# Two normalisation stages of a two-layer network, their orders of work written anew

## The reference, cut to what matters

```python
m = jnp.mean(x, axis=channels); v = jnp.var(x, axis=channels)
xn = (x - m) / jnp.sqrt(v + eps)                          # normalise, eps 1e-6
x_proj = jnp.einsum('bchw,mc->bmhw', xn, w_in)            # 128 -> 16 channels
s = x + xn
...                                                       # FFT, gain, inverse FFT of x_proj: x_enh (16 channels)
x1 = s + jnp.einsum('bmhw,cm->bchw', x_enh, w_out)        # 16 -> 128 channels
tn = (x1 - mean(x1)) / jnp.sqrt(var(x1) + eps)            # eps 1e-5
total[c, b] = sum over the points of tn                   # for the router of the experts
```

## Time and profile before

| | |
|---|---|
| median of three runs | 3659.25 us (3657.81 to 3667.75) |
| the profiled execution's own time | 3660.29 us |
| its span, first to last instruction | 3658.5 us |
| TensorE busy, share of the span | 87% |
| VectorE, ScalarE, GpSimd | 46%, 42%, 22% |
| mean granted TensorE clock | 0.903 of full |

### The profile page before, as it was taken

The page is one execution under the profiler, slowest core; times in us unless marked ns, Lnnn a source line. Parts: engine busy times, 40 slices in busy tenths (PEclk is TensorE's granted clock), DMA queues, the critical chain, the costliest instruction groups (busy, mean ns, idle before and its releaser), DMA issues. The chain is left out here.

```text
span 3658.5 us, 67013 instructions
## 1 busy us (share of the span) xinstructions
PE 3166.6 (87%) x27077; PEld 1711.9 (47%) x27136; DVE 1684.6 (46%) x2348; ACT 1527.2 (42%) x2263; POOL 810.3 (22%) x694
## 2 busy tenths in 40 slices
PE   5655676399999985999997879999999999999999
PEld 1155422255555542566665434546463545545444
DVE  5724256567677541111112254545454645545453
ACT  3411244167776661111223334545453444445433
POOL 2410232134444421111110112121212111121221
PEclk7767666699999985999998889999999999999999
DMA  5421364313334323777777311313132231313000
GB/s 187 154 75 23 121 257 196 157 46 138 147 147 164 153 115 123 187 212 214 214 207 236 123 56 52 127 46 128 51 104 81 76 109 41 110 43 125 12 12 23
DMA packets 192538, 438.59 MB, mean 120 GB/s; under 512 B 33341, under 2 KB 100157, under 8 KB 183741
## 3 DMA queue, kind: packets, MB, share of 16 engines
q1 hardware_dynamic: 192356, 436.20, 35.9%
HBM read 247.40 MB, written 188.75 MB: 119 GB/s over the span
## 5 line engine op out<-in xcount | busy, mean ns | idle before, releaser
L2113 DVE TENSOR_TENSOR d_hid_scaled<-d_hid_scaled,d_ps 128x512 f32<-128x512 f32 x512 | 331.3, 684 | 605.7 <-PE d_ps L1800 553.6
L1789 PE MATMUL d_ps<-d_hid_scaled,d_w 128*128 128x512 f32 x1024 | 526.4, 596 | 8.0 <-DVE d_X L2119 3.8
L1974 ACT ACTIVATE d_hid_scaled<-d_ps,d_b 128x512 f32<-128x512 f32 x512 | 349.9, 686 | 382.0 <-PE d_ps L1778 375.6
L1517 PE MATMUL c_ps<-c_pad,c_weight 32*32 32x512 f32 x13824 | 475.2, 601 | 26.2 <-ACT c_pad L1469 18.9
L1517 PEld LDWEIGHTS c_ps<-c_pad,c_weight 32*32 32x32 f32 x13824 | 287.1, 103 | 214.1 <-issue 129.7
L1776 PE MATMUL d_ps<-d_tnh,d_w1h 128*128 128x512 f32 x512 | 296.5, 579 | 9.2 <-ACT d_hid_scaled L1974 9.2
L1148 PE MATMUL b_ps<-b_hid,b_w2s 128*128 128x512 f32 x512 | 261.6, 595 | 0.0
L2061 POOL CAST d_tnh<-d_TN 128x512 fp32r<-128x512 f32 x64 | 39.9, 623 | 972.7 <-PE d_ps L1778 935.4
L1578 DVE COPY c_pad<-c_P 128x1024 f32<-128x1024 f32 x48 | 33.4, 696 | 414.9 <-PE c_ps L1517 379.2
L1789 PEld LDWEIGHTS d_ps<-d_hid_scaled,d_w 128*128 128x128 f32 x1024 | 195.5, 191 | 44.5 <-DVE d_hid_scaled L2113 2.3
L1469 ACT ACTIVATE c_pad<-c_P 128x1024 f32<-128x1024 f32 x48 | 51.8, 1080 | 392.7 <-PE c_ps L1517 372.0
(11 more groups left out here) (270 smaller groups left out, 5858.7 us busy)
## 6 DMA issues: line engine op xcount, KB each, us to landing
scratch_qkv<-b_qkv SPq DMA_DIRECT2D x64, 768.0 KB, 3.5
c_P<-scratch_qkv SPq DMA_DIRECT2D x192, 256.0 KB, 4.7
scratch_agg<-c_out SPq DMA_DIRECT2D x192, 256.0 KB, 5.0
d_buf<-scratch_qkv SPq DMA_DIRECT2D x96, 512.0 KB, 4.4
d_buf<-scratch_agg SPq DMA_DIRECT2D x96, 512.0 KB, 3.8
p_X<-in_x SPq DMA_DIRECT2D x8, 2048.0 KB, 7.5
scratch_s<-p_X SPq DMA_DIRECT2D x8, 2048.0 KB, 6.3
m_X<-scratch_s SPq DMA_DIRECT2D x8, 2048.0 KB, 7.7
```

Source lines behind the costliest of these rows:

```text
L1517: end = nc.tensor.matmul(ps[on(i), k * QUADS + h, :].rearrange("p (b r w) -> p b r w", b=2, w=HB), weight[k][on(q), 2 * r + x, on(h)], pad ...
L1789: nc.tensor.matmul(moe_bank, w2[:, e, :], scaled[n % 3][:, :], start=False, stop=(e == E - 1)).then_inc(moe_pe, 1)
L1974: nc.scalar.activation(hid[n % 3][:, :], hid_bank(n), ACT.Gelu, bias=b1[:, n % E:n % E + 1]).then_inc(hid_done, 1)
L2113: nc.vector.tensor_tensor(scaled[n % 3][:, :], hid[n % 3][:, :], spread_bank(n), ALU.mult).then_inc(scaled_done, 1)
```

## The change

Both stages get new orders; the arithmetic is the same. In the projection stage the squares have eight buffers; `variances` is cut in two halves that stand behind `cast_inverse` 0 to 3 and 4 to 7, `means(b+1)` stands behind both, and `project` and `read` work on image b-2 and stand last; ScalarE does `deviations` before `split(b+1,0)`; VectorE does all eight `scale` before `invert`. In the mix stage `X` and `XE` hold four images; `mix` runs two images ahead and in pairs between the groups of casts and sums; `means(b+1)` stands behind the first four `cast_mean(b)`; `split(b-1,1)` and `join(b-1,1)` move to the next turn, the join behind `centre(b)`; `join(b+1,0)` stands before `invert(b)`. SyncE loads four images ahead, and stores `x1` of b+2 in turn b.

```diff
 # projection stage
-        norm = TileNorm(nc, ctx, "p_norm", ..., [t[:, :] for t in banks[2:6]])
+        norm = TileNorm(nc, ctx, "p_norm", ..., [t[:, :] for t in banks[2:6]], NCH)
...
                     for c in range(NCH):
                         norm.cast_mean(pe, b, c, mean_free(b))
+                    for c in range(4):
+                        norm.cast_inverse(pe, b - 1, c, inverse_free(b - 1))
+                    norm.variances(pe, b, range(4))
+                    for c in range(4, NCH):
+                        norm.cast_inverse(pe, b - 1, c, inverse_free(b - 1))
+                    norm.variances(pe, b, range(4, NCH))
                     if more:
                         means(b + 1)
-                    for c in range(4):
-                        norm.cast_inverse(pe, b - 1, c, inverse_free(b - 1))
-                    norm.variances(pe, b)
-                    for c in range(4, NCH):
-                        norm.cast_inverse(pe, b - 1, c, inverse_free(b - 1))
-                    project(b - 1)
+                    if b >= 2:
+                        project(b - 2)
...
                 body(B - 1, False)
                 for c in range(NCH):
                     norm.cast_inverse(pe, B - 1, c, inverse_free(B - 1))
+                project(B - 2)
                 project(B - 1)
...
                     for c in range(NCH):
                         norm.squares(act, b, c, xn_part(b), lambda c: norm.wait_centred(act, b, c))
+                    norm.deviations(act, b, eps)
                     if more:
                         norm.split(act, b + 1, 0)
-                    norm.deviations(act, b, eps)
                     norm.split(act, b, 1)
+                    if b >= 2:
+                        read(b - 2)
...
                 for b in range(1, B - 1):
                     body(b, True)
-                    read(b - 1)
...
                     centre(b)
-                    scale(b - 1, range(6))
+                    scale(b - 1, range(NCH))
                     norm.invert(dve, b)
-                    scale(b - 1, range(6, NCH))
 # mix stage
-        X, TN, XE = sb("X", [128, 3 * HW]), sb("TN", [128, 3 * HW]), sb("XE", [128, 3 * ROWS])
+        X, TN, XE = sb("X", [128, 4 * HW]), sb("TN", [128, 3 * HW]), sb("XE", [128, 4 * ROWS])
...
                 load(0)
-                for b in (1, 2):
+                for b in range(1, 4):
                     sp.wait_ge(loaded, b * 80)
                     load(b)
                 store_x1(0)
...
+                sp.wait_ge(x1_stored, 16)
+                store_x1(1)
+                for b in range(B):
+                    if b + 4 < B:
+                        next_load(b)
+                    if b + 2 < B:
+                        sp.wait_ge(x1_stored, b * 16 + 32)
+                        store_x1(b + 2)
+                    if b:
+                        store_tn(b - 1)
...
+                for b in range(2):
+                    for i in range(NCH):
+                        mix(b, i)
+                    if b == 0:
+                        means(0)
+                def mixes(b, some):
+                    for i in some:
+                        if b < B:
+                            mix(b, i)
+
+                for b in range(B):
+                    for c in range(4):
                         norm.cast_mean(pe, b, c, mean_free(b))
-                        if more:
-                            mix(b + 1, c)
...
+                    if b + 1 < B:
+                        means(b + 1)
+                    mixes(b + 2, (0, 1))
+                    for c in range(4, NCH):
+                        norm.cast_mean(pe, b, c, mean_free(b))
+                    mixes(b + 2, (2, 3))
+                    if b:
+                        for c in range(4):
+                            norm.cast_inverse(pe, b - 1, c, inverse_free(b - 1))
+                    mixes(b + 2, (4, 5))
+                    norm.variances(pe, b)
+                    mixes(b + 2, (6, 7))
+                    if b:
+                        for c in range(4, NCH):
+                            norm.cast_inverse(pe, b - 1, c, inverse_free(b - 1))
                 for c in range(NCH):
                     norm.cast_inverse(pe, B - 1, c, inverse_free(B - 1))
...
+                for b in range(B):
+                    if b:
+                        norm.split(act, b - 1, 1)
+                    squares(b, (0, 1))
+                    if b + 1 < B:
+                        norm.split(act, b + 1, 0)
+                    reads(b + 2, (0, 1))
+                    squares(b, (2, 3, 4))
+                    reads(b + 2, (2, 3))
+                    squares(b, (5, 6, 7))
+                    reads(b + 2, (4, 5))
                     norm.deviations(act, b, eps)
+                    reads(b + 2, (6, 7))
+                norm.split(act, B - 1, 1)
...
+                norm.join(dve, 0, 0)
+                for b in range(B):
                     centre(b)
-                    scale(b - 1, range(6))
+                    if b:
+                        norm.join(dve, b - 1, 1)
+                        scale(b - 1, range(NCH))
+                    if b + 1 < B:
+                        norm.join(dve, b + 1, 0)
                     norm.invert(dve, b)
-                    scale(b - 1, range(6, NCH))
-                    norm.join(dve, b, 1)
...
+                norm.join(dve, B - 1, 1)
                 scale(B - 1, range(NCH))
```

More of the change, by code:

```diff
@@ L740, in phase_mix @@
         y_pe, y_done, x1_done, total_done, total_stored = sem("y_pe"), sem("y_done"), sem("x1_done"), sem("total_done"), sem("total_stored")
-        third = lambda buf, b: buf[:, bass.ds((b % 3) * HW, HW)]
-        part = lambda buf, b: lambda c: buf[:, bass.ds((b % 3) * HW + c * CH, CH)]
+        image = lambda b: X[:, b % 4 * HW:(b % 4 + 1) * HW]
+        normed = lambda b: TN[:, b % 3 * HW:(b % 3 + 1) * HW]
+        x_part = lambda b: lambda c: chunk(image(b), c)
+        tn_part = lambda b: lambda c: chunk(normed(b), c)
+        rows = lambda b: slice(b % 4 * ROWS, (b % 4 + 1) * ROWS)
         ORDER = [chunk_of(g, w) for w in range(2) for g in range(4)]
@@ L752, in load @@
                 def load(b):
-                    sp.dma_start(third(X, b), batch_of(d["s"], b)).then_inc(loaded, 16)
+                    sp.dma_start(image(b), batch_of(d["s"], b)).then_inc(loaded, 16)
                     for g in range(4):
-                        sp.dma_start(XE[32 * g:32 * g + MID, bass.ds((b % 3) * ROWS, ROWS)],
+                        sp.dma_start(XE[32 * g:32 * g + MID, rows(b)],
                                      d["xe"][bass.ds(b, 1), :, g * ROWS:(g + 1) * ROWS].rearrange("a m n -> (a m) n")).then_inc(loaded, 16)
@@ L760, in store_x1 @@
                     passed(sp)
-                    sp.dma_start(batch_of(d["x1"], b), third(X, b)).then_inc(x1_stored, 16)
+                    sp.dma_start(batch_of(d["x1"], b), image(b)).then_inc(x1_stored, 16)
                 def store_tn(b):
@@ L771, in next_load @@
                     norm.wait_centred(sp, b, NCH - 1)
-                    sp.wait_ge(loaded, b * 80 + 240)
-                    passed(sp)
-                    load(b + 3)
+                    sp.wait_ge(loaded, b * 80 + 320)
+                    load(b + 4)
                 load(0)
-                for b in (1, 2):
+                for b in range(1, 4):
                     sp.wait_ge(loaded, b * 80)
@@ L831, in means @@
                     pe.wait_ge(x1_done, b * NCH + NCH + 4)
-                    norm.means(pe, b, part(X, b))
-                def body(b, more):
-                    for c in range(NCH):
-                        norm.cast_mean(pe, b, c, mean_free(b))
-                        if more:
-                            mix(b + 1, c)
-                    for c in range(4):
-                        norm.cast_inverse(pe, b - 1, c, inverse_free(b - 1))
-                    norm.variances(pe, b)
[L842 to L857, removed]
+                    norm.means(pe, b, x_part(b))
+                for b in range(2):
[9 more added lines that the diff above has]
+                    for c in range(4):
+                        norm.cast_mean(pe, b, c, mean_free(b))
+                    if b + 1 < B:
[8 more added lines that the diff above has]
+                    mixes(b + 2, (4, 5))
+                    norm.variances(pe, b)
+                    mixes(b + 2, (6, 7))
+                    if b:
+                        for c in range(4, NCH):
+                            norm.cast_inverse(pe, b - 1, c, inverse_free(b - 1))
                 for c in range(NCH):
@@ L871, in read, with squares, reads @@
                     nc.scalar.activation(Y[i % 4][:, :], banks[6 + i % 2][:, :], ACT.Copy).then_inc(y_done, 1)
[L873 to L877, removed]
-                    norm.deviations(act, b, eps)
[L879 to L888, removed]
+                for b in range(2):
+                    for i in range(NCH):
+                        read(b, i)
```

(30 more changed lines are left out.)

16 lines of the change are left out of this document (3 added, 13 removed).

## The result

The changed kernel takes 3611.74 us in the median (3607.3 to 3615.43, four runs), the one before beside it 3663.5 us. The ratio is 0.9857, with a 95% interval of 0.9832 to 0.9882, so some 52 us less (9 either way). Both stages gave: the projection stage lasts 170.3 us instead of 211.3, the mix stage, from its first DMA to that of the stage behind, 220.5 instead of 234.3.

A forecast was written before the change was run, and what follows sets the result against it. Both stages were taken as bound by chains of waits, with no engine full. From 3660.3 us, 36.6 (projection) and 9.3 (mix) come off, 3614.4, or 3613 against the median; 80% range 3590 to 3638.

The forecast's parts named there:

- VectorE decides in turns 1 and 2, 16.1 us each: Projection stage: VectorE's own work sets these two turns, 16.1 us instead of 22.3, 12.4 us gained.
- The reciprocal can start by C+9.9: Projection stage: with C the start of `centre(b)`, sums and root allow the reciprocal by 9.9 us after it.
- The load chain decides from image 4 on, 18.3 us: Projection stage: load, means, project, read and `pm` stores take 18.3 us between load landings; total stage gain 36.6 us.
- the sign that the prediction gave: Projection stage profile: TensorE's `means` waits for `p_X` from DMA, 1 to 3 us a turn, turns some 18 us.
- The first image gains 3.5: Projection stage, image 0: it loses its 5.1 us wait for squares, 3.5 us gained, centre 1 at 32.9.
- The mix turn is 21.8: Mix stage: TensorE's chain with joins at 1.4 us and half the possible clock gain; 21.8 us a turn, gain 9.3 us.
- the bounds of 18.6 to 23.9: Mix turn: 18.6 us with all 4.0 us of clock gain and joins at 0.75; 23.9 us as upper bound.
- The stages behind do the same: After the two changed stages: the later stages start later by nothing and do the same.
- (1): Rival, mix stage: clock stays low and joins wait, turn 23.9 us or a little more; 3626 us, chance 0.17.
- (2): Rival, mix stage: TensorE at full clock through most of the turn, 18.6 us; 3595 us, chance 0.08.
- (3): Rival, projection stage: longer load chain as stores and load share engines, turn 22 us; 3628 us, chance 0.09.
- (4): Rival, projection stage: load waits out the `s` and `pm` stores, slower than before; 3672 us at turns of 33, chance 0.04.

The follow-up runs named there:

- e7: Changed kernel with the projection stage's sums of squares in one block behind cast 7; projection stage 177.3 us, median 3611.2 us.
- e9: Changed kernel with each of the four `pm` stores cut in two, same bytes in eight stores; projection stage 178.2 us, median 3620.4 us.
- e10: e4 with each of the four `pm` stores cut in two; projection stage 170.0 us, median 3611.0 us.
- e3: Changed kernel with the projection stage's squares in four buffers again; projection stage 176.0 us, median 3617.6 us.
- e5: Changed kernel with the second part of each split in PSUM, so joins read one SBUF operand; stages 168.7 and 215.3 us, median 3601.0 us.
- e4: Changed kernel with project and read on image b-1 instead of b-2; projection stage 170.3 us, median 3607.9 us.
- e8: Changed kernel with the edits of e4 and e5 together; stages 166.6 and 215.2 us, median 3598.6 us.
- e6: Changed kernel with each mix on 128 rows of TensorE instead of 16, zeros in the other weight rows; mix stage 222.0 us, median 3610.8 us.

## Why the prediction was right

The forecast, 3613 us, is 1.3 us off the median, and that close it is by luck. The two stages gave 54.7 us and not 45.9. In the profiled execution 9.8 us went back elsewhere, 7.8 of them in the first experts' stage, and the kernel before took 3663.5 beside this one and not the 3659 that the forecast is set against, so that by the medians the gain is 52 us against 46 forecast. By its own steps:

- **VectorE decides in turns 1 and 2, 16.1 us each.** Right as a mechanism, measured 16.35 and 16.65 (centres at 33.27, 49.62 and 66.27). Inside, two terms were off, and partly cancelled. "The reciprocal can start by C+9.9" was C+11.0, since the first half of the sums, at the lower clock, holds up casts 4 to 7 (the 1.15 us hole), and the second half took 1.94 us where 1.1 to 1.8 were taken; and the two joins took 2.37 and not 3.0. In the turn shown VectorE's own scales and the sums' root end within 0.1 us of each other, and e7 shows what a later end of the sums costs.
- **The load chain decides from image 4 on, 18.3 us.** This is the step that was mis-sized. The four `pm` stores were taken at 3.98 from a row in which they follow the store of `s`; apart from it they took 1.73. Means was taken at 3.2 and ran in 2.0 to 2.4, since it now stands straight behind the sums. With 1.73 and 2.04 the prediction's terms add up to 14.4 us. They leave out the splits that ScalarE has ahead of the read: in the turn shown the reads end at 82.91, 6.7 us behind the start of means, and 1.2 of these are a wait for the reciprocal. So VectorE's turn of 16.7 us set when the loads went out. Loads 4 to 6 landed 16.9 and 16.6 us apart, 0.3 to 0.4 us ahead of their means, so the sign that the prediction gave, means waiting 1 to 3 us a turn from turn 3 on, didn't come. Only the last load was late (turn 6: 17.7), with the store of `s` issued 0.5 us behind it, as the prediction had said. e9 and e10 show the chain and how close it was. Gain 41.0 instead of 36.6, and under the 45 that the prediction named for faster stores and turns of 16.1.
- **The first image gains 3.5.** Centre 1 at 33.27 against 36.43: 3.2. e3 shows that it comes from the buffers (36.21 there).
- **The mix turn is 21.8.** Measured 21.2 over five turns; the bounds of 18.6 to 23.9 hold every turn (19.9 to 23.6). That the joins would take about 1.4 us beside GpSimd was right: they took 0.88 to 1.78 in these turns, 1.3 in the mean, and e5 took it away. The clock gave back about what was taken for it: 0.59 to 0.67, and in the one turn at 0.50 the 23.7 us come close to the prediction's 23.9 for the lower clock throughout. The gain was 13.7 instead of 9.3, five turns of 0.6 less and the rest in the first and last.
- **The stages behind do the same.** No run ties a difference there to the change. From one profile to another the first experts' stage differs by 8 us, which the prediction didn't know.

Of the rivals, (1) and (2) would have needed mix turns of 23.9 and 18.6. One turn came near the first at 23.6, and the shortest was 19.9. (3) and (4) needed load turns of 22 us and above 32; the longest was 17.7, and 20.1 with the dearer stores of e9.

## What to carry to other kernels

Cost a DMA issue from a row in which it stands behind the same neighbours as it will: the same four stores cost 1.7 or 4 us, and e9, with 3.6 us for them, shows the load behind them become the critical chain. A wait's total in the profile is no gain: 40 us of ScalarE's waits were worth 6, because the sums that they delayed were due later; find what ends last behind the wait. When an order is changed, look at which two-input VectorE operations come beside GpSimd's work, and give one input a place in PSUM: it took the joins from up to 1.78 us to 0.75.

## What the runs showed of the hardware

- Four stores of 64 KB from 16 partitions each took SyncE 1.7 to 2.0 us to issue, and 3.7 to 4.6 us when a 2 MB store was issued 0.5 to 2.2 us before (before, changed kernel, e4, e8). No run varies this distance by itself.
- TensorE's granted clock rose from between 0.50 and 0.67 to 0.78 in the turns of the mix stage when the mixes used 128 rows instead of 16 and ran one after the other (e6), at the same number of instructions. The Trainium skill, TensorE: Matmul & The Clock Gate, Loop structure matters more than you think, says that matmuls back to back keep the clock up. The runs don't fit that alone: with 17.8 of 23.5 us at work it was 0.78 on 128 rows, with 18.4 of 23.7 it was 0.50 on 16.
- The first experts' stage, the same code in twelve profiles, took 782 us in five and 788 to 791 in seven, with a granted clock of 0.96 to 0.97 or of 0.58 in the same 21 us stretch.
